# Laying out the context and three weight matrices by columns on the host, in a gated cross-attention and expert kernel

## The chip, the cores and the metric

The kernel runs on one core of a Trainium2 chip. The metric is device microseconds of one execution, the median of several runs. The engines are called TensorE (PE in the rows; PEld is its weight load), VectorE (DVE), ScalarE (ACT), GpSimd (POOL) and the DMA queue of the Sync engine (SP).

## What is computed

Inputs are `x` and a context, both (8, 512, 512) in float32: 8 batches of 512 rows and 512 features. Cut to what matters:

```python
n = layernorm(x); c = ctx_1024
s  = softmax((n @ Wq_c.T + bq_c) @ (c @ Wk_s.T + bk_s).T / sqrt(512)) @ (c @ Wv_s.T + bv_s)   # d = 0
t  = softmax((c @ Wq_s.T + bq_s) @ (n @ Wk_c.T + bk_c).T / sqrt(512)) @ (n @ Wv_c.T + bv_c)   # d = 1
g  = sigmoid(concat([s, t]) @ Wg.T + bg)
x  = x + tanh(g_xattn) * (g * s + (1 - g) * t)
m  = layernorm(x)
p  = softmax(m @ router_w + router_b);  e = argmax(p)
x  = x + tanh(g_ffn) * max(p) * (m @ expert_w[e] + expert_b[e])                                # 8 experts
```

## The kernel before

**Number format.** Every operand of a large product is kept as a pair, a high part (a rounded copy, made by ScalarE) and a low part (value minus high part, made by VectorE). `product` (L153) multiplies two pairs over four chunks of 128 in three passes: 12 matmuls of 128x512. The pairs live in an arena of nine slots of [128, 2, 4, 512]: `WG_S, A_X, A_C, CT, XT, WV_S, WV_C, WG_C, PAIRS` (L56). CT and XT hold the context and the normalised x of one batch with the features across the partitions, so they need the transposed inputs. WV_S, WV_C, WG_C and WG_S need the transposed weights.

**Steps.** The work of all engines is written out by hand as one list of steps (`opening_steps` L180, `steps_of_a_batch` L496, `steps_after` L584). Each engine walks the same list and does its part of each step, in that order; semaphores join them. A step is a kind and digits: Q10 is kind Q, direction 1, tile 0. Kinds: Q (queries, product with the folded matrix A = Wk.T Wq), S (scores, with the row maximum on VectorE and the exponential on ScalarE), NP (normalisation), V (values), PT (transposes of the probabilities), U (attended sum, into four banks), ND, G (gate), M, MX, BS, NM, NT, NR, LG, LR (mix, statistics and router logits of the batch before), RT, RK (ranks for the expert lists), XS, XN, XD, XT (x of the next batch: statistics, normalisation, a dot product, transposes), CD, CT (context of the next batch: a dot product, transposes). Only in the first batch come the steps of the weights: W (splits), AC, AD, A (products for the folded matrices) with AE (their eviction), SC (a scaled copy on ScalarE, added up by GpSimd, L361), FOLD0 to FOLD2 (sums over that, which the first scores and dot products need) and WT0 to WT15 (the transposed weights, four tiles each of WG_C, WV_S, WV_C, WG_S in this order, `LATE` L57).

The first batch runs as written out code, batches 1 to 6 in a hardware loop (L1132, L1245, L1437), the last again as written out code, and behind it 39 expert tiles.

**A CT, XT or WT step before.** Four transposes by TensorE into one bank (`transposes` L1003; CT L1085, WT L1082), a copy of the bank to the high part by ScalarE (L1199, L1209), a subtraction by VectorE to the low part (L1277, called at L1333 and L1337). In the loop CT0 stands behind Q13, CT1 and CT2 between the scores of direction 1, and CT3 between V11 and PT11. The source of CT is the same `in_tile` that CD reads; SP waits for both in front of the next load into it (`after_c` L834).

**WT loads before.** SP loads 16 tiles of 256 KB one after the other into four small tiles (`late_rows` L648, L935 to L940), each as soon as the transposes of the one four places before are done.

**Gates that the steps below touch.** V of the first batch waits for the low parts of WV (L1026), U00 for the second folded matrix (L1048), S00 for CT's low parts and FOLD2 (L1031 to L1033), FOLD1 and FOLD2 for GpSimd's additions (L471), PT10 for the normalised probabilities (L1040).

Of the kernel before, what the change touches and what calls it, by code (L numbers as in the profile page):

```python
# [73 lines left out]
def gated_attention_and_experts(nc, x, ctx_in, g_xattn, g_ffn, Wq_c, bq_c, Wk_s, bk_s, Wv_s, bv_s,  # L74
                                Wq_s, bq_s, Wk_c, bk_c, Wv_c, bv_c, Wg, bg, router_w, router_b,
                                expert_w, expert_b, out):
# [8 lines left out]
    with ExitStack() as top:  # L85
# [90 lines left out]
WT_ROWS = 4  # L176
# [15 lines left out]
def weights_part(nc, top, k, x1_dram, list_dram, w):  # L192
# [297 lines left out]
    part.nat_lo, part.scaled_up, part.fold_read = nat_lo, scaled_up, fold_read  # L490
# [114 lines left out]
def attention_part(nc, scope, top, k, x_rows, c_rows, x1_dram, x1_early, list_dram, expert_w,  # L605
# [163 lines left out]
    def tr_bank_of(step):  # L769
# [3 lines left out]
        if kind in ("M", "WT") or kind in ("NT", "CT", "XT") and rel == 0:  # L773
            return tr_bank[i % 2]
# [25 lines left out]
    def wait_readers(pe, b, step):  # L800
# [12 lines left out]
        elif kind == "CT":  # L813
            pe.wait_ge(ct_lo, per_batch(b + rel, i))
# [6 lines left out]
        elif kind == "RK":  # L821
            pe.wait_ge(ranks_read, b + rel + 1)
        elif kind == "WT":
            pe.wait_ge(wt_lo, i + 1)

    def sync(sp, weights_run, experts_run):
# [7 lines left out]
        def after_c(b, t):  # L834
            await_count(sp, waits_passed_sp, ct_tr, per_batch(b, t))
# [1050 lines left out]
```

## Time and profile before

| what | value |
|---|---|
| median of 3 runs | 1160.65 us (1157.68 to 1161.5) |
| the profiled execution | 1168.7 us, span 1166.9 us |
| mean granted TensorE clock | 0.999 |
| TensorE matmuls busy | 1146.8 us, 98% of the span |
| TensorE weight loads busy | 943.5 us, 81% |
| VectorE, ScalarE, GpSimd busy | 709.8, 458.8, 212.4 us (61, 39, 18%) |
| DMA | 90.64 MB, mean 78 GB/s |

The span reaches from the first to the last instruction of the profiled execution. "Busy" is the time in which at least one instruction of the engine is under way; matmuls overlap, so their durations add up to more than the time they take. In a timeline row the bracket at the end is idle time of the engine in front of the row, and who ended it.

### The profile page before, as it was taken

What the parts mean: (1) busy time and instruction counts of PE and PEld (TensorE: products, weight loads), DVE (VectorE), ACT (ScalarE), POOL (GpSimd) and SP (SyncE); (2) the same over time, 40 slices, a digit from 0 to 9 for tenths busy, and PEclk for the clock granted to TensorE, in tenths of its full rate; (3) what the DMA queues carried; (4) which work ended last, traced back from release to release, by engine and by line L of the source; (5) the groups of instructions that cost most, each with busy time, mean ns of one, the idle gap of its engine ahead of it and who ended that gap; (6) DMA issues with size and microseconds to landing.
All of it is one profiled execution on the core that took longest, in us unless ns stands there. A gap on an engine that the chain in (4) does not pass through costs nothing.

```text
span 1166.9 us, 18111 instructions
## 1 busy us (share of the span) xinstructions
PE 1146.8 (98%) x5933; PEld 943.5 (81%) x5933; DVE 709.8 (61%) x1494; ACT 458.8 (39%) x815; POOL 212.4 (18%) x339
## 2 busy tenths in 40 slices
PE   8999999999999999999999999999999999998998
PEld 7878888888888888888888888888888888876776
DVE  6666646564656565654576366646664667787565
ACT  5634413442343234432443234423442344553332
POOL 2400101020102000210011001101120102165564
PEclk9999999999999999999999999999999999999999
DMA  7141103011201020102011111112000322685683
GB/s 254 49 162 37 37 28 100 19 31 36 99 0 48 27 99 9 48 27 81 27 39 34 56 54 21 36 42 84 21 28 10 136 62 66 221 266 167 187 252 109
DMA packets 59445, 90.64 MB, mean 78 GB/s; under 512 B 20523, under 2 KB 21063, under 8 KB 59401
## 3 DMA queue, kind: packets, MB, share of 16 engines
q1 hardware_dynamic: 49232, 64.25, 18.2%
q0 software_dynamic: 7264, 19.20, 5.1%
q10 hardware_dynamic: 2904, 6.63, 1.6%
q8 instruction: 24, 0.39, 0.1%
q14 instruction: 21, 0.16, 0.0%
HBM read 62.77 MB, written 29.12 MB: 79 GB/s over the span
## 4 chain that ended last, share of the span: by engine, by line
PE 93%; issue 3%; SPq 2%; DVE 1%; ACT 1%; DMA 0%; another core or an unknown queue 0%; POOL 0%; POOLq 0%; DVEq 0%
PE mm L160 59%; PE u L1053 15%; PE tr L1005 8%; PE u L160 6%; PE tr L160 1%; PE mm L1834 1%; PE u L443 1%; SPq L1583 1%; PE tr L1107 1%; SPq L1584 1%; PE mm L485 0%; DMA probs<-in_L_ffn_expert_b 0%; SPq L1604 0%; SPq L1603 0%; DVE slot_as_f L1810 0%
## 5 line engine op out<-in xcount | busy, mean ns | idle before, releaser
L160 PE MATMUL mm<-arena 128*128 128x512 f32 x1536 | 374.2, 395 | 1.5 <-DVE arena L1277 1.4
L160 PEld LDWEIGHTS mm<-arena 128*128 128x128 f32 x1536 | 282.8, 188 | 58.6 <-DVE arena L1277 1.7
L1053 PE MATMUL u<-arena 128*128 128x512 f32 x768 | 189.8, 397 | 0.0
L160 PE MATMUL mm<-arena,q_pair 128*128 128x512 f32 x768 | 183.8, 394 | 0.0
L160 PEld LDWEIGHTS mm<-arena,q_pair 128*128 128x128 f32 x768 | 141.7, 188 | 28.7
L1053 PEld LDWEIGHTS u<-arena 128*128 128x128 f32 x768 | 140.0, 188 | 27.4
L1277 DVE TENSOR_TENSOR arena<-tr,arena 128x512 fp32r<-128x512 f32 x143 | 96.1, 686 | 36.6 <-ACT arena L1168 16.5
L1277 DVE TENSOR_TENSOR arena<-mm,arena 128x512 fp32r<-128x512 f32 x65 | 45.0, 692 | 91.6 <-ACT arena L1159 87.2
L1155 ACT ACTIVATE q_pair<-mm,c_col 128x512 fp32r<-128x512 f32 x64 | 44.1, 689 | 125.8 <-PE mm L160 122.6
L1278 DVE SCALAR_TENSOR_TENSOR q_pair<-mm,c_col,q_pair 128x512 fp32r<-128x512 f32 x64 | 48.1, 751 | 70.7 <-ACT q_pair L1155 69.1
L1159 ACT ACTIVATE arena<-mm 128x512 fp32r<-128x512 f32 x64 | 38.3, 599 | 128.8 <-PE mm L160 128.8
L160 PE MATMUL mm<-c2s_pair,arena 128*128 128x512 f32 x360 | 87.2, 392 | 0.0
L160 PE MATMUL mm<-q_pair,arena 128*128 128x512 f32 x360 | 86.4, 389 | 0.0
L1164 ACT ACTIVATE probs<-mm,neg_top 128x512 f32<-128x512 f32 x64 | 44.2, 690 | 102.4 <-DVE neg_top L1304 92.8
L160 PE MATMUL u<-arena,q_pair 128*128 x312 | 79.4, 405 | 1.3 <-DVE q_pair L1795 1.2
L1461 POOL TENSOR_SCALAR mv_x<-mv_x 128x1 f32<-128x1 f32 x28 | 12.6, 451 | 368.1 <-DVE mv_x L1344 368.1
L160 PEld LDWEIGHTS mm<-q_pair,arena 128*128 128x128 f32 x360 | 67.6, 188 | 14.0
L160 PEld LDWEIGHTS mm<-c2s_pair,arena 128*128 128x128 f32 x360 | 67.1, 188 | 13.8
L1461 POOL TENSOR_SCALAR stats<-stats 128x1 f32<-128x1 f32 x32 | 8.0, 248 | 355.9 <-DVE stats L1376 355.6
L1323 DVE SCALAR_TENSOR_TENSOR probs<-probs,u 128x512 f32<-128x512 f32 x32 | 22.0, 688 | 79.4 <-ACT probs L1191 79.2
L1191 ACT ACTIVATE probs<-mm,bg_half 128x512 f32<-128x512 f32 x30 | 20.7, 690 | 123.6 <-PE mm L160 123.6
L160 PEld LDWEIGHTS u<-arena,q_pair 128*128 128x128 f32 x312 | 57.9, 192 | 13.4 <-issue 2.0
(223 smaller groups left out, 1558.8 us busy)
## 6 DMA issues: line engine op xcount, KB each, us to landing
in_tile<-in_ctx SPq DMA_DIRECT2D x31, 256.0 KB, 2.7
x_tile<-in_x SPq DMA_DIRECT2D x29, 256.0 KB, 2.6
x_rows<-x_tile SPq DMA_DIRECT2D x29, 256.0 KB
in_tile<-in_x SPq DMA_DIRECT2D x28, 256.0 KB, 2.6
x_rows_early<-x_tile SPq DMA_DIRECT2D x28, 256.0 KB, 2.3
probs<-in_L_ffn_expert_b SPq DMA_DIRECT2D x21, 256.0 KB
slot_as_f<-in_L_ffn_expert_w SPq DMA_DIRECT2D x4, 1024.0 KB, 5.3
slot_as_f<-in_L_ffn_expert_w ACTq DMA_DIRECT2D x3, 1024.0 KB, 7.6
```

The lines of the kernel that those rows point to most:

```text
L160: last = pe.matmul(bank, lhsT(a, c), rhs(b, c), start=start and n == 0, stop=stop and n == C * len(PASSES) - 1)
L443: last = pe.matmul(bank[m][:], pair[0][0][:, a, i, m * P:(m + 1) * P], pair[0][1][:, b, i], start=i == 0 and n == 0, stop=i == C - 1 and n ...
L1005: last = pe.transpose(bank[:, tile(n)], block_of(n), ident[:])
L1053: last = pe.matmul(u_bank[m][:], v_pair[:, i % 2, a, tile(m)], pt_pair[:, i % 2, p], start=i == 0 and n == 0, stop=i == T - 1 and n == 2)
L1155: act.activation(q_pair[:, HI, i], bank[:], ACT.Identity, bias=c_col[:, d, i:i + 1]).then_inc(q_hi, 1)
L1159: act.activation(v_pair[:, i % 2, HI], bank[:], ACT.Copy).then_inc(v_hi, 1)
L1164: act.activation(probs[:, i], bank[:], ACT.Exp, bias=neg_top[:, d, i:i + 1], scale=SCALE, accum_out=p_sum[:, d, i:i + 1]).then_inc(exp_don ...
L1191: act.activation(probs[:, i], bank[:], ACT.Tanh, bias=bg_half[:, i:i + 1], scale=0.5).then_inc(tanh_done, 1)
L1277: return dve.tensor_tensor(to, bank, f32(hi), ALU.subtract)
L1278: return dve.scalar_tensor_tensor(to, bank, bias, f32(hi), ALU.add, ALU.subtract)
L1323: dve.scalar_tensor_tensor(mix, mix, 1.0, u_bank[i][:], ALU.subtract, ALU.mult).then_inc(nd_used, 1)
L1461: then(pool.tensor_scalar(rstd, var, EPS, None, ALU.add))
```

## The change

The host hands over the context transposed in each batch (`ctx_1024_by_columns`, beside the context itself) and `Wv_s`, `Wv_c` and `Wg` transposed (in place of the originals). A plain DMA puts them where TensorE's transposes and the two evictions put them before:

- `load_columns_of_c` loads the context of one batch, 1 MB, straight into the low half of the CT slot (for batch 0 of the WG_S slot). It waits until the last Q of direction 1 is done; in the loop it stands on SP behind `store_stats` and in front of `load_rest_of_x`.
- `load_late` loads each of the four weight blocks, 1 MB each, into the low half of its own slot (WV_S into the four small tiles), each behind a wait of its own.
- ScalarE copies from there to the high half, VectorE subtracts in place. TensorE's part of CT and WT, their banks and their waits are gone. SP's `after_c` waits for the dot product alone.
- CT0 to CT3 of the next batch move back in the list: behind U10, U11, U12 and U13. In the first batch, CT of batch 0 and all WT steps stay in their places.

The core of the diff (signatures, names of semaphores and argument lists left out):

```diff
@@ steps_of_a_batch
-    s += cur("Q", 1, 3) + load(6, 7) + nxt("CT", 0)
+    s += cur("Q", 1, 3) + load(6, 7)
     keep = lambda *ns: [("KC", 0, 0, n) for n in ns]
-    s += nxt("XN", 0) + cur("S", 1, 0) + prev("RK", 0) + nxt("CT", 1) + keep(0)
-    s += cur("S", 1, 1) + keep(1) + nxt("XD", 0) + cur("S", 1, 2) + nxt("CT", 2) + keep(2)
+    s += nxt("XN", 0) + cur("S", 1, 0) + prev("RK", 0) + keep(0)
+    s += cur("S", 1, 1) + keep(1) + nxt("XD", 0) + cur("S", 1, 2) + keep(2)
     s += cur("S", 1, 3) + keep(3) + cur("NP", 1, 3) + table(0) + nxt("CD", 2) + cur("V", 1, 0)
     s += nxt("XT", 0) + load(8) + cur("PT", 1, 0) + load(9)
-    s += cur("V", 1, 1) + load(10) + nxt("CD", 3) + nxt("CT", 3) + cur("PT", 1, 1) + table(1) + load(11, 12) + cur("U", 1, 0)
-    s += load(13) + nxt("XS", 1)
-    s += cur("V", 1, 2) + load(14) + nxt("XN", 1) + cur("PT", 1, 2) + table(2) + load(15) + cur("U", 1, 1) + nxt("XS", 2) + nxt("XD", 1)
+    s += cur("V", 1, 1) + load(10) + nxt("CD", 3) + cur("PT", 1, 1) + table(1) + load(11, 12) + cur("U", 1, 0)
+    s += load(13) + nxt("CT", 0) + nxt("XS", 1)
+    s += cur("V", 1, 2) + load(14) + nxt("XN", 1) + cur("PT", 1, 2) + table(2) + load(15) + cur("U", 1, 1) + nxt("CT", 1)
+    s += nxt("XS", 2) + nxt("XD", 1)
...
-    s += nxt("XS", 3) + prev("ID", 0) + nxt("XD", 2) + nxt("XT", 2) + nxt("XN", 3)
+    s += nxt("CT", 2) + nxt("XS", 3) + prev("ID", 0) + nxt("XD", 2) + nxt("XT", 2) + nxt("XN", 3)
...
-    s += cur("U", 1, 3)
+    s += cur("U", 1, 3) + nxt("CT", 3)
@@ attention_part
+    def columns_of_c(b, i):
+
+        slot = WG_S if isinstance(b, int) and b == 0 else CT
+        return k.slot_as_f32[slot][:, LO, i]
+
+    def late_raw(i):
+
+        return late_rows[i % C] if LATE[i // C] == WV_S else k.slot_as_f32[LATE[i // C]][:, LO, i % C]
@@ sync
         def after_c(b, t):
-            await_count(sp, waits_passed_sp, ct_tr, per_batch(b, t))
             await_count(sp, waits_passed_sp, c_dotted, per_batch(b, t))
+        def load_columns_of_c(b, first=False):
+            if first:
+                sp.wait_ge(weights.group_mm, C)
+            else:
+                await_count(sp, waits_passed_sp, q_mm, per_dir(b - 1, 1, C - 1))
+            to = k.slot_as_f32[WG_S if first else CT][:, LO]
+            sp.dma_start(to, ctx_columns[bass.ds(b, 1)].rearrange("o (c p) l -> p (o c) l", p=P)).then_inc(ct_loaded, 16)
+
+        def load_late(n):
+            place, w = LATE[n], late_weights[n]
+            if place == WV_S:
+                for c in range(C):
+                    sp.dma_start(late_rows[c], w[tile(c), :]).then_inc(wt_loaded[n], 16)
+                return
+            if place == WG_C:
+                sp.wait_ge(weights.nat_lo, 2 * C)
+                sp.wait_ge(weights.folded_col, C)
+            elif place == WV_C:
+                sp.wait_ge(weights.group_mm, 2 * C)
+            else:
+                sp.wait_ge(ct_lo, C)
+            sp.dma_start(k.slot_as_f32[place][:, LO], w.rearrange("(c p) o -> p c o", p=P)).then_inc(wt_loaded[n], 16)
...
         load_small()
+        load_late(LATE.index(WV_S))
+        load_late(LATE.index(WG_C))
+        load_columns_of_c(0, first=True)
         sp.wait_ge(in_loaded[0], loads_of("C", 0, 0))
-        sp.wait_ge(weights.group_mm, C)
         load_c(0, T - 1)
-        for n in range(4 * C):
-            if n == 11:
-                load_next(1, first=True)
-            if n >= WT_ROWS:
-                sp.wait_ge(wt_tr, n - WT_ROWS + 1)
-            sp.dma_start(late_rows[n % WT_ROWS], late_weights[n // C][tile(n % C), :]).then_inc(wt_loaded[n % WT_ROWS], 16)
-        sp.wait_ge(wt_tr, 4 * C)
+        load_late(LATE.index(WV_C))
+        load_late(LATE.index(WG_S))
+        load_next(1, first=True)
+        sp.wait_ge(wt_lo, C * (LATE.index(WV_S) + 1))
         load_first_residual(0)
         load_rest_of_c(1)
+        load_columns_of_c(1)
         load_rest_of_x(1)
...
             load_rest_of_c(b + 1)
             store_stats(b - 1)
+            load_columns_of_c(b + 1)
             load_rest_of_x(b + 1)
@@ tensor
-                elif kind == "WT":
-                    pe.wait_ge(wt_loaded[i % WT_ROWS], 16 * (i // WT_ROWS + 1))
-                    transposes(bank, lambda n: late_rows[i % WT_ROWS][:, tile(n)]).then_inc(wt_tr, 1)
-                elif kind == "CT":
-                    buf = place_of("C", bb, i)
-                    pe.wait_ge(in_loaded[buf], loads_of("C", bb, i))
-                    transposes(bank, lambda n: c_of(bb, i)[:, tile(n)]).then_inc(ct_tr, 1)
@@ scalar
+                elif kind == "CT":
+                    act.wait_ge(ct_loaded, 16 * (bb + 1))
+                    if first and rel == 0 and i == 0:
+                        act.wait_ge(weights.nat_lo, 4 * C)
+                        act.wait_ge(weights.scaled_up, 3 * C)
+                    act.activation(arena[:, CT, HI, i], columns_of_c(bb, i), ACT.Copy).then_inc(ct_hi, 1)
                 elif kind == "WT":
...
                         lists_filled()
+                        act.wait_ge(c_dotted, T)
                     if i == 0:
                         act.wait_ge(weights.scaled_up, C)
-                    act.wait_ge(wt_tr, i + 1)
-                    act.activation(arena[:, LATE[i // C], HI, :, tile(i % C)],
-                                   bank[:].rearrange("p (c t) -> p c t", c=C), ACT.Copy).then_inc(wt_hi, 1)
+                    if LATE[i // C] == WV_S and i % C == 0:
+                        act.wait_ge(weights.group_mm, 2 * C)
+                    act.wait_ge(wt_loaded[i // C], 16 * (C if LATE[i // C] == WV_S else 1))
+                    act.activation(arena[:, LATE[i // C], HI, i % C], late_raw(i), ACT.Copy).then_inc(wt_hi, 1)
@@ vector
+                elif kind == "CT":
+                    dve.wait_ge(ct_hi, per_batch(bb, i))
+                    low(arena[:, CT, LO, i], columns_of_c(bb, i), arena[:, CT, HI, i]).then_inc(ct_lo, 1)
                 elif kind == "WT":
                     dve.wait_ge(wt_hi, i + 1)
-                    low(arena[:, LATE[i // C], LO, :, tile(i % C)], bank[:].rearrange("p (c t) -> p c t", c=C),
-                        arena[:, LATE[i // C], HI, :, tile(i % C)]).then_inc(wt_lo, 1)
+                    low(arena[:, LATE[i // C], LO, i % C], late_raw(i),
+                        arena[:, LATE[i // C], HI, i % C]).then_inc(wt_lo, 1)
```

## Rows read from the trace of the kernel before

**Rows 1.** The page: TensorE's busy time, and its granted clock by slice.

```profile
PE 1146.8 (98%) x5933; PEld 943.5 (81%) x5933; DVE 709.8 (61%) x1494; ACT 458.8 (39%) x815; POOL 212.4 (18%) x339
...
PEclk9999999999999999999999999999999999999999
```

**Rows 2.** The page: the chain that ended last, by engine.

```profile
PE 93%; issue 3%; SPq 2%; DVE 1%; ACT 1%; DMA 0%; another core or an unknown queue 0%; POOL 0%; POOLq 0%; DVEq 0%
```

**Rows 3.** Windows by stage: us, busy (count) by engine, PEclk, DMA share, GB/s.

```profile
65.70:91.99 26.29, 26.29 (x133) 21.84 (x134) 15.74 (x32) 10.85 (x20) 0.00 (x0) 1.00 0.30 99
...
204.53:937.40 732.87, 732.87 (x3834) 605.76 (x3832) 428.21 (x932) 271.41 (x488) 84.80 (x174) 1.00 0.14 44
...
1060.00:1166.90 106.90, 94.56 (x452) 75.58 (x450) 65.15 (x117) 35.65 (x55) 60.73 (x58) 0.98 0.61 179
```

**Rows 4.** Line 1005: count, duration ns min/median/max, first and last start.

```profile
L1005 PE MATMUL tr<-ident,in_tile x236: 270/272/308, 41.9 to 880.7; 128*128 128x128 f32 x118
```

**Rows 5.** TensorE in time, loop, from Q13's end (start us, us, what).

```profile
225.97 0.60 PE L1005 MATMUL tr<-ident,in_tile 128*128 128x128 f32 x4
...
235.50 0.60 PE L1005 MATMUL tr<-ident,in_tile 128*128 128x128 f32 x4
...
238.71 1.52 PE L160 MATMUL mm<-arena 128*128 128x512 f32 x6
```

**Rows 6.** TensorE in time, last batch, S10 and V10.

```profile
958.80 2.88 PE L160 MATMUL mm<-arena,q_pair 128*128 128x512 f32 x12
...
970.14 2.88 PE L160 MATMUL mm<-arena 128*128 128x512 f32 x12
```

**Rows 7.** TensorE in time, loop, CT3 and PT11.

```profile
245.04 0.60 PE L1005 MATMUL tr<-ident,in_tile 128*128 128x128 f32 x4
245.48 0.60 PE L1005 MATMUL tr<-ident,probs 128*128 128x128 f32 x4
```

**Rows 8.** VectorE's lines 1348 and 1394, GpSimd's 361: ns min/median/max.

```profile
L1348 DVE CUSTOM_DVE_ANT_0 junk<-pairs_as_f,u_row,u_const x4: 752/1200/1824, 40.7 to 50.3; 128x512 bf16<-128x512 f32 x4
...
L1394 DVE TENSOR_TENSOR arena<-slot_as_f,arena x32: 681/684/694, 929.6 to 1015.6; 128x512 fp32r<-128x512 f32 x32
...
L361 POOL TENSOR_TENSOR slot_as_f<-slot_as_f x9: 1278/1297/1740, 33.3 to 44.9; 128x512 f32<-128x512 f32 x9
```

**Rows 9.** SP in time, the page's loads (KB, us to landing), ScalarE in time.

```profile
232.24 0.41 SPq L871 DMA_DIRECT2D x_rows<-stats  x1
...
slot_as_f<-in_L_ffn_expert_w SPq DMA_DIRECT2D x4, 1024.0 KB, 5.3
...
251.59 0.60 ACT L1159 ACTIVATE arena<-mm 128x512 fp32r<-128x512 f32 x1 [4.77 <-PE mm L160]
```

**Rows 10.** First batch in time: FOLD1, FOLD2, S00 on TensorE; GpSimd's additions.

```profile
37.57 0.35 PE L479 MATMUL mm<-slot_as_f 128*128 128x1 f32 x2 [0.38 <-issue]
...
46.44 0.95 PE L476 MATMUL mm<-slot_as_f 128*128 128x1 f32 x8
...
51.52 3.00 PE L160 MATMUL mm<-arena,q_pair 128*128 128x512 f32 x12
...
33.29 4.18 POOL L361 TENSOR_TENSOR slot_as_f<-slot_as_f 128x512 f32<-128x512 f32 x3 [14.98 <-ACT slot_as_f L295]
...
40.65 5.50 POOL L361 TENSOR_TENSOR slot_as_f<-slot_as_f 128x512 f32<-128x512 f32 x4 [0.26 <-ACT slot_as_f L295]
```

**Rows 11.** First batch's S phase in time: row maxima, WT7's subtraction, V00.

```profile
54.63 0.69 DVE L1300 TENSOR_REDUCE mx<-mm 128x1 f32<-128x512 f32 x1 [0.76 <-PE mm L160]
...
58.85 0.68 DVE L1300 TENSOR_REDUCE mx<-mm 128x1 f32<-128x512 f32 x1
...
62.46 0.68 DVE L1300 TENSOR_REDUCE mx<-mm 128x1 f32<-128x512 f32 x1
...
64.86 0.69 DVE L1277 TENSOR_TENSOR arena<-tr,arena 128x512 fp32r<-128x512 f32 x1 [0.74 <-ACT arena L1209]
...
65.70 3.01 PE L160 MATMUL mm<-arena 128*128 128x512 f32 x12
```

More of the change, by code:

```diff
@@ L71, in f32, with gated_attention_and_experts @@
     return ap.bitcast(F32)
-def gated_attention_and_experts(nc, x, ctx_in, g_xattn, g_ffn, Wq_c, bq_c, Wk_s, bk_s, Wv_s, bv_s,
-                                Wq_s, bq_s, Wk_c, bk_c, Wv_c, bv_c, Wg, bg, router_w, router_b,
-                                expert_w, expert_b, out):
+def gated_attention_and_experts(nc, x, ctx_in, g_xattn, g_ffn, Wq_c, bq_c, Wk_s, bk_s, bv_s,
+                                Wq_s, bq_s, Wk_c, bk_c, bv_c, bg, router_w, router_b,
+                                expert_w, expert_b, ctx_columns, Wv_s_columns, Wv_c_columns, Wg_columns, out):
     x_rows = x.rearrange("b l h -> (b l) h")
@@ L126, in gated_attention_and_experts @@
         with ExitStack() as scope:
-            attention = attention_part(nc, scope, top, k, x_rows, c_rows, x1_dram, x1_early, list_dram, expert_w,
-                                       (Wg[:, 0:H], Wv_s, Wv_c, Wg[:, H:2 * H]), weights)
+            attention = attention_part(nc, scope, top, k, x_rows, c_rows, ctx_columns, x1_dram, x1_early, list_dram,
+                                       expert_w, (Wg_columns[0:H, :], Wv_s_columns, Wv_c_columns,
+                                                  Wg_columns[H:2 * H, :]), weights)
         experts = experts_part(nc, top, k, x1_dram, x1_early, list_dram, out_rows, expert_b, attention)
@@ L489, in weights_part @@
     part = Part(sync, scalar, vector, gpsimd, tensor)
-    part.nat_lo, part.scaled_up, part.fold_read = nat_lo, scaled_up, fold_read
+    part.nat_lo, part.scaled_up, part.fold_read, part.folded_col = nat_lo, scaled_up, fold_read, folded_col
     part.group_mm, part.group_lo, part.router_split = group_mm, group_lo, router_split
@@ L660, in attention_part @@
     q_mm, v_mm, s_mm, u_mm, g_mm = sem("q_mm"), sem("v_mm"), sem("s_mm"), sem("u_mm"), sem("g_mm")
-    pt_tr, ct_tr, xt_tr, m_tr, nt_tr = sem("pt_tr"), sem("ct_tr"), sem("xt_tr"), sem("m_tr"), sem("nt_tr")
+    pt_tr, xt_tr, m_tr, nt_tr = sem("pt_tr"), sem("xt_tr"), sem("m_tr"), sem("nt_tr")
+    ct_loaded = sem("ct_loaded")
     lg_mm, rk_mm, gc_mm = sem("lg_mm"), sem("rk_mm"), sem("gc_mm")
     lg_read = sem("lg_read")
-    wt_loaded, wt_tr, wt_hi, wt_lo = [sem(f"wt_loaded{i}") for i in range(WT_ROWS)], sem("wt_tr"), sem("wt_hi"), sem("wt_lo")
+    wt_loaded, wt_hi, wt_lo = [sem(f"wt_loaded{i}") for i in range(C)], sem("wt_hi"), sem("wt_lo")
     ex_loaded, ex_hi, ex_lo = [sem(f"ex_loaded{i}") for i in range(E + 1)], sem("ex_hi"), sem("ex_lo")
@@ L721, in c_of @@
         if isinstance(b, int) and b == 0 and t == T - 1:
-            return k.slot_as_f32[WG_S][:, LO, 0]
+            return k.slot_as_f32[WG_S][:, HI, C - 1]
         return in_tile[:, place_of("C", b, t), 0:H]
+    def columns_of_c(b, i):
[3 more added lines that the diff above has]
+        return late_rows[i % C] if LATE[i // C] == WV_S else k.slot_as_f32[LATE[i // C]][:, LO, i % C]
     def x_is_loaded(engine, b, t):
@@ L772, in tr_bank_of @@
             return mm_bank[1]
-        if kind in ("M", "WT") or kind in ("NT", "CT", "XT") and rel == 0:
+        if kind == "M" or kind in ("NT", "XT") and rel == 0:
             return tr_bank[i % 2]
@@ L1192, in run @@
                                    scale=0.5).then_inc(tanh_done, 1)
-                elif kind in ("CT", "XT"):
-                    done, hi, to = (ct_tr, ct_hi, CT) if kind == "CT" else (xt_tr, xt_hi, XT)
-                    act.wait_ge(done, per_batch(bb, i))
-                    if first and kind == "CT" and rel == 0 and i == 0:
+                elif kind == "XT":
+                    act.wait_ge(xt_tr, per_batch(bb, i))
+                    act.activation(arena[:, XT, HI, :, tile(i)], bank[:].rearrange("p (c t) -> p c t", c=C),
+                                   ACT.Copy).then_inc(xt_hi, 1)
+                elif kind == "CT":
+                    act.wait_ge(ct_loaded, 16 * (bb + 1))
+                    if first and rel == 0 and i == 0:
                         act.wait_ge(weights.nat_lo, 4 * C)
                         act.wait_ge(weights.scaled_up, 3 * C)
-                    act.activation(arena[:, to, HI, :, tile(i)], bank[:].rearrange("p (c t) -> p c t", c=C),
-                                   ACT.Copy).then_inc(hi, 1)
+                    act.activation(arena[:, CT, HI, i], columns_of_c(bb, i), ACT.Copy).then_inc(ct_hi, 1)
                 elif kind == "WT":
@@ L1517, in attention_part @@
     part.x1_copied, part.stats_copied = x1_copied, stats_copied
-    part.tiles_read = (xt_tr, x_dotted, ct_tr, c_dotted)
+    part.tiles_read = (xt_tr, x_dotted, c_dotted)
     part.m_tr, part.probs = m_tr, probs
@@ L1877 @@
     arrays, args = {}, []
-    for name in _INS:
-        a = _np.ascontiguousarray(inputs[name])
-        arrays[f"in_{name}"] = a
-        args.append(nc.dram_tensor(f"in_{name}", a.shape, _mybir.dt.from_np(a.dtype), kind="ExternalInput").ap())
+    laid_out = [(f"in_{name}", _np.ascontiguousarray(inputs[name])) for name in _INS]
+    laid_out += [(f"in_{name}_by_columns", _np.ascontiguousarray(_np.swapaxes(_np.asarray(inputs[name]), -1, -2)))
+                 for name in _INS_BY_COLUMNS]
+    for name, a in laid_out:
+        arrays[name] = a
+        args.append(nc.dram_tensor(name, a.shape, _mybir.dt.from_np(a.dtype), kind="ExternalInput").ap())
     args.append(nc.dram_tensor("out", (B, L, H), _mybir.dt.float32, kind="ExternalOutput").ap())
```

25 lines of the change are left out of this document (10 added, 15 removed).

## The prediction, made before the changed kernel had run

> **What bounds the kernel now.** I read the page's busy times and slices first. TensorE's matmul row is busy 98% of the span at a granted clock of 9 tenths or more in every slice [rows 1], and the chain that ended last is TensorE for 93% [rows 2]. The windows by stage say more than the averages: from 204.53 to 937.40 us, six batches, TensorE is busy 732.87 of 732.87 us while VectorE is busy 428 and ScalarE 271; in the last 107 us it is busy 94.6, so only the ends have gaps [rows 3]. In the batch loop, therefore, whatever is taken out of TensorE's stream comes off the time, as long as no partner that it stops covering becomes late. In the first batch that has to be checked wait by wait.
>
> **What a removed group is worth.** A CT or WT step is four 128x128 transposes into one bank. Their rows say 272 ns each [rows 4], but they are pipelined, so what counts is the distance between starts. The same stretch of steps, Q13's end to V10's start, stands in the loop with CT0, CT1 and CT2 in it and in the last batch (which has no next one) without. In the loop it goes from 225.97 to 238.71, 12.74 us [rows 5]. In the last batch S10 starts at 958.80 and V10 at 970.14, 11.34 us, with the same four products and the same ranks step [rows 6]. The difference, 1.40 us, is three groups: 0.467 us each, some 0.35 of issue and 0.11 that the product behind transposes takes longer. CT3 stands next to PT11, so it costs only the distance to it, 245.48 - 245.04 = 0.44 us [rows 7]. One batch's CT steps: 1.40 + 0.44 = 1.84 us.
>
> Weighed against that: durations would give 192 x 0.272 = 52 us, where distances give 48 x 0.46 = 22. The Trainium skill ("TensorE: Matmul & The Clock Gate", Part 4: PE-mode transpose) gives about 275 ns for a transpose in a kernel's context; taken as a cost that would make 52.8 us. The pair of stretches decides for the distance.
>
> **Part by part.**
> - *CT of batches 1 to 7, in the loop's code.* 28 groups leave TensorE: 7 x 1.84 = 12.9 us. What they covered: with CT0 gone S10 follows Q13 at once, and its last third needs Q13's low half; in the last batch that same adjacency runs without a gap [rows 6]. S12 and S13 now also stand back to back, as there. In this phase VectorE loses three subtractions and TensorE 1.40 us, so its cover improves. I cost the loss at 0 and keep for the range one group per batch, 7 x 0.467 = 3.3 us.
> - *CT0 to CT3 moved behind U10, U11, U12 and U13 on ScalarE and VectorE.* Each is one ScalarE copy and one VectorE subtraction as before, now with SBUF sources. The expert weights are split by just these forms: the subtraction takes 684 ns [rows 8]. ScalarE is idle 4.77 us in front of V12's eviction, so CT0 fits there [rows 9]. CT3 puts 0.7 us in front of the ND steps, with TensorE busy on the gate products for some 22 us. Cost 0.
> - *The load of the columns.* One 1 MB transfer per batch on SP, behind the stores of the statistics, issued at 232.24 in the batch shown [rows 9]; the column load follows at about 233.3. A 1 MB expert load takes a median 5.3 us to land [rows 9], so it is there at about 239. ScalarE reaches CT0 at 246.8 (251.59 less the idle 4.77): 8 us of cover. The three x loads behind it on SP wait for steps that come later (XT0 after V10, then CD2 and CD3), so they are not held. The former wait for the transposes in front of the next loads falls away. 8 MB more over the kernel, where the loop moves 44 GB/s and has its DMA engines 14% busy [rows 3]. Cost 0; if the cover is gone, see the slower rival.
> - *The first batch, up to FOLD2.* Seven groups (WT0, WT1, CT0 to CT3, WT2) are worth 7 x 0.45 = 3.1 us on TensorE, but GpSimd gates two places. FOLD1 started at 37.57, 0.1 us after GpSimd's third addition ended (33.29 + 4.18 = 37.47) and after 0.38 us of idle: it can't come sooner, so WT0 is lost. FOLD2 started at 46.44 and needs the last addition, which ended at 40.65 + 5.50 = 46.15 [rows 10]. So FOLD2 gains at most some 0.3 us, plus 0.3 if GpSimd's own gap is closed, though five more groups ahead of it are gone. Only WT2 lies behind it. Best case: 0.5 + 0.4 = 0.9 us. Against it, the subtractions now read two SBUF operands while GpSimd adds: with one such operation beside it, VectorE took up to 1.82 us for a form that takes 0.75, and one of GpSimd's nine additions took 1.74 us instead of 1.30 [rows 8]. Six subtractions now fall between 35 and 46 us; at 0.1 to 0.4 us each GpSimd ends 0.6 to 2.4 us later. I take 0.7 us. Net at S00 (51.52 before): +0.2 us gained, between -1.5 and +0.9. The Trainium skill ("GPSIMD Engine Reference", 1. Specifications) says that GpSimd's SBUF interfaces are contended by VectorE instructions with two SBUF inputs; it speaks against this change, and the trace agrees. Without that rule the stretch would gain 0.9.
> - *The first batch's S phase.* WT3 to WT7 are five groups, 2.2 us. But V00 waits for WT7's subtraction: it ran from 64.86 to 65.55, and V00 started at 65.70 [rows 11]. Behind that stands a chain through ScalarE and VectorE: each row maximum started 3.2 to 4.2 us after the one before (54.63, 58.85, 62.46), where a product takes 2.73 us. In program order lie maximum, exponential on ScalarE, the WT copies behind it, their subtractions, next maximum; no link of it waits for a transpose. Taking 5 groups out of TensorE leaves it. Gain 0.1 us, at most 2.2.
> - *WT8 to WT15.* From V00 on TensorE has no idle time (26.29 of 26.29 us in the window behind it [rows 3]): 8 x 0.44 = 3.5 us, less some 0.3 because U00 starts close behind the second fold's last subtraction. 3.2 us.
> - *The weight loads.* WG_C and batch 0's columns are issued once the first matrices are split, near 25 us, and are needed at 35 and 43 us; two times 5.3 us lands them near 36 at the latest, and the first WT copy is ScalarE's, not TensorE's. WV_C and WG_S land long before WT8 and WT12. Cost 0, up to 1 us.
> - *Last batch and experts.* Nothing is removed; their waits are for things that move along with the last batch. 0.
>
> **Sum.** 12.9 + 0.2 + 0.1 + 3.2 = 16.4 us. Against the profiled execution's span of 1166.9 (1168.7 us with what lies around it) that is 1.4%. The median of the runs shown is 1160.65, 0.7% below the profiled one; at this size the scaling is worth 0.1 us. Forecast: 1160.65 - 16.4 = **1144.2 us**.
>
> **Rivals.**
> - *All 48 groups come off.* 22.1 us, 1138.6. For it: TensorE's 98%. Against it: the gates of FOLD2 and V00 [rows 10, 11]. Chance 0.14.
> - *A partner becomes late somewhere.* The opening loses 1.5 instead of gaining 0.2, and one group per batch is swallowed in the loop's S phase (VectorE has a dot product there that the last batch lacks): 16.4 - 1.7 - 3.3 = 11.4 us, 1149.2; either alone 1146 to 1147.5. Chance 0.16.
> - *The transposes cost their durations.* 52 us, 1108.5. The equal stretches speak against it. Chance 0.01.
> - *Slower: the column load lands late.* ScalarE waits in order at CT0, behind it stands V12's eviction, and TensorE stops at the next product into that bank. It needs landing later than 13.5 us after issue to be felt on ScalarE, another 4.8 us before it delays the eviction, and then 16.4 / 7 = 2.3 us per batch to eat the gain: decides at some 20.6 us from issue, four times 5.3. At 25 us it would cost 7 x (25 - 18.3) = 47 us less the 16: 1191. Chance 0.04.
> - *Nothing to be seen (under 3.5 us gained).* It would need two thirds of a batch's groups swallowed in every batch; also if the 3 runs' own spread of 3.8 us hides part. Chance 0.05.
>
> **How the numbers follow.** My forecast has 0.60. About 0.3% (3.5 us) is what a measurement of this kernel can tell from no change. Faster by more: 0.60 + 0.14 + 0.16 + 0.01 = 0.91; same 0.05; slower 0.04. The range reaches from just below the case with all groups, 1138, to the case with the partners late, 1150.
>
> **What would show it.** Right: six batches take 732.9 - 6 x 1.84 = 721.8 us with TensorE still busy throughout, and the distance of S10 to V10 is the last batch's 11.3 us; FOLD2 starts between 46 and 48 us with idle time in front of it; V00 still waits for a subtraction of WT7 near 65.5; GpSimd's additions last longer. Wrong: idle time of TensorE in every batch (then who released it is the answer), FOLD2 near 44 us, V00 near 61, ScalarE waiting for the transfer of the columns at CT0, or a batch that shrinks by less than 1.5 us.

## The result and the profile after

The changed kernel takes 1147.09 us (median of 4 runs, 1145.39 to 1149.16), the kernel before 1159.54 (4 runs, 1157.68 to 1161.5): a ratio of 0.9893, 95% interval 0.9867 to 0.9919, or 12.4 us less. The forecast was 16.4 us less, from 1160.65 to 1144.2. The profiled execution has a span of 1146.1 us. One of the six executions of e4 below took 1896.96 us at a mean granted clock of 0.556; it is left out of the times and ratios here.

The page's rows of the changed kernel: busy times, granted clock by slice, chain of waits by engine, and the new load (count, KB each, median us to landing).

```profile
PE 1126.0 (98%) x5741; PEld 925.1 (81%) x5741; DVE 708.2 (62%) x1494; ACT 460.8 (40%) x815; POOL 209.8 (18%) x339
...
PEclk9999999999999999999999999999999999999999
...
PE 88%; issue 3%; SPq 2%; POOL 2%; DVE 2%; DMA 2%; ACT 1%; POOLq 0%; ACTq 0%; DVEq 0%
...
slot_as_f<-in_ctx_by_columns SPq DMA_DIRECT2D x8, 1024.0 KB, 5.6
```

TensorE is as full as before [rows 1], but the chain that ended last goes through it for 88% instead of 93% [rows 2]: the rest now passes through GpSimd, VectorE and DMA. Where that is shows in the windows of TensorE (us, busy and count, granted clock, DMA share, GB/s), first six batches of the loop, then three stretches of the first batch.

```profile
203.76:925.42 721.66, 721.66 (x3733) 1.00 0.18 54
...
44.00:48.00 4.00, 1.93 (x10) 1.00 0.01 4
48.00:52.00 4.00, 4.00 (x15) 0.63 0.00 0
...
68.00:72.00 4.00, 3.37 (x10) 0.69 0.13 50
```

The six batches take 721.66 us (721.8 forecast) instead of those of [rows 3], without any idle time: the loop gives what it was to give. The first batch doesn't. Between 44 and 48 us TensorE is busy 1.93 of 4 us, and behind that the granted clock is 0.63 and 0.69, where the kernel before showed a full clock throughout its first batch.

The loop, on TensorE's timeline: S10 and V10, to be set beside [rows 5, 6].

```profile
225.01 2.88 PE L161 MATMUL mm<-arena,q_pair 128*128 128x512 f32 x12
...
236.35 2.88 PE L161 MATMUL mm<-arena 128*128 128x512 f32 x12
```

11.34 us, the very distance of the last batch in [rows 6]; it was 12.74. The column load and its use, SP's queue and ScalarE's copy for CT0 and eviction of V12:

```profile
232.12 0.40 SPq L895 DMA_DIRECT2D slot_as_f<-in_ctx_by_columns  x1
```

```profile
243.89 0.64 ACT L1225 ACTIVATE arena<-slot_as_f 128x512 fp32r<-128x512 f32 x1
248.84 0.60 ACT L1182 ACTIVATE arena<-mm 128x512 fp32r<-128x512 f32 x1 [4.32 <-PE mm L161]
```

Issued at 232.12, landed 5.6 us later by the median, first used at 243.89: 6 us of cover, and ScalarE still idles 4.32 us in front of V12's eviction. No ScalarE or TensorE wait goes back to this load.

The opening, on TensorE's timeline from FOLD0 to PT00 (the bracket is idle time in front and who ended it).

```profile
25.89 0.95 PE L476 MATMUL u<-slot_as_f 128*128 128x1 f32 x8
...
39.11 0.35 PE L479 MATMUL mm<-slot_as_f 128*128 128x1 f32 x2 [1.24 <-issue]
...
47.99 1.05 PE L476 MATMUL mm<-slot_as_f 128*128 128x1 f32 x8 [2.07 <-POOL slot_as_f L361]
...
50.30 4.32 PE L161 MATMUL u<-arena 128*128 128x512 f32 x12
54.46 8.32 PE L161 MATMUL mm<-arena,q_pair 128*128 128x512 f32 x36
63.64 3.03 PE L161 MATMUL mm<-arena,q_pair 128*128 128x512 f32 x12 [0.86 <-ACT probs L1187]
68.63 4.57 PE L161 MATMUL mm<-arena 128*128 128x512 f32 x12 [1.95 <-DVE arena L1304]
...
73.04 0.60 PE L1035 MATMUL tr<-ident,probs 128*128 128x128 f32 x4
```

In order: FOLD0, FOLD1, FOLD2, A13, the scores S00 to S02, S03, V00, PT00. A13 and its successor in the kernel before, on TensorE's timeline:

```profile
48.02 3.32 PE L160 MATMUL u<-arena 128*128 128x512 f32 x12
...
51.17 0.60 PE L1005 MATMUL tr<-ident,normed 128*128 128x128 f32 x4
```

Against these and [rows 10, 11] three things are new. FOLD2 waits 2.07 us for GpSimd. A13 behind it takes 4.16 us to its successor (50.30 to 54.46), where it took 3.15. V00 waits 1.95 us for the subtraction of WT7, and then takes 4.4 us itself. Both slow products lie in the windows with the low clock above. The wait in front of FOLD1 grew as well, from 0.38 to 1.24 us: the place of the transposes is empty, and FOLD1 comes 13.22 us behind FOLD0 instead of 12.85.

### The profile page after: what moved, and what is told of

It reads as the page before. It is cut to its first block, busy times and chain, and to the rows that moved or that the text cites. A ratio compares the mean times of both kernels' runs of the same rounds, so it can differ in the third digit from the quotient of the medians.

```text
span 1146.1 us, 17654 instructions
## 1 busy us (share of the span) xinstructions
PE 1126.0 (98%) x5741; PEld 925.1 (81%) x5741; DVE 708.2 (62%) x1494; ACT 460.8 (40%) x815; POOL 209.8 (18%) x339
## 4 chain that ended last, share of the span: by engine, by line
PE 88%; issue 3%; SPq 2%; POOL 2%; DVE 2%; DMA 2%; ACT 1%; POOLq 0%; ACTq 0%; DVEq 0%
PE mm L161 59%; PE u L1083 15%; PE tr L1035 6%; PE u L161 4%; PE tr L161 1%; SPq L1612 1%; PE tr L1130 1%; DMA in_tile<-x_rows,u_row 1%; SPq L1613 1%; POOL slot_as_f L361 1%; PE mm L1863 1%; POOL out L1692 1%; DMA pairs_as_f<-in_x 0%; DMA probs<-in_L_ffn_expert_b 0%; DVE slot_as_f L1839 0%
## 5 line engine op out<-in xcount | busy, mean ns | idle before, releaser
L161 PE MATMUL mm<-arena,q_pair 128*128 128x512 f32 x768 | 179.7, 391 | 0.9 <-ACT probs L1187 0.9
L1304 DVE TENSOR_TENSOR arena<-tr,arena 128x512 fp32r<-128x512 f32 x95 | 63.9, 685 | 20.2 <-ACT arena L1191 16.4
L1327 DVE TENSOR_REDUCE mx<-mm 128x1 f32<-128x512 f32 x64 | 44.2, 691 | 50.9 <-PE mm L161 50.8
```

The costliest lines, as they stand in the source:

```text
L161: last = pe.matmul(bank, lhsT(a, c), rhs(b, c), start=start and n == 0, stop=stop and n == C * len(PASSES) - 1)
L1304: return dve.tensor_tensor(to, bank, f32(hi), ALU.subtract)
L1327: then(dve.reduce_max(mx[:, d, i:i + 1], bank[:], axis=AX))
```

## Where the time went, by stage

Starts of the same steps in each profiled execution, subtracted (us). The labels are those of the experiments below; e0 is the changed kernel again. The experiments ran on three chips: e1 to e4 on one, e0 and e5 to e7 on a second, e8 and e9 on a third. The kernel before ran beside them on each and took 1167.5 to 1167.6 us, 8 us more than in the first comparison, so what is compared below is the ratio to it. e9 is e6 once more and left out here.

| stage | before | after | e0 | e1 | e2 | e3 | e4 | e5 | e6 | e7 | e8 |
|---|---|---|---|---|---|---|---|---|---|---|---|
| FOLD0 to FOLD2 | 21.72 | 22.10 | 22.05 | 22.09 | 22.08 | 21.27 | 21.70 | 22.08 | 21.71 | 24.47 | 21.73 |
| FOLD2 to S00 | 5.08 | 6.47 | 6.44 | 5.21 | 8.09 | 6.47 | 5.07 | 4.82 | 4.72 | 3.25 | 4.72 |
| S00 to V00 | 14.18 | 14.17 | 14.16 | 14.28 | 14.17 | 14.17 | 14.19 | 14.17 | 11.45 | 11.56 | 11.45 |
| V00 to PT00 | 2.85 | 4.41 | 4.05 | 2.85 | 2.83 | 4.26 | 2.85 | 2.83 | 2.85 | 2.81 | 2.85 |
| **FOLD0 to PT00** | **43.83** | **47.15** | **46.70** | **44.43** | **47.17** | **46.17** | **43.81** | **43.90** | **40.73** | **42.09** | **40.75** |
| PT00 to S10, batch 0 | 36.00 | 32.16 | 32.21 | 32.18 | 32.14 | 32.20 | 35.61 | 32.16 | 32.16 | 32.16 | 32.16 |
| S10 to the last gate | 895.15 | 882.38 | 882.46 | 882.59 | 882.76 | 882.66 | 882.76 | 882.43 | 883.25 | 883.47 | 883.26 |
| last gate to the end | 167.20 | 158.52 | 166.14 | 161.83 | 164.07 | 166.45 | 162.98 | 165.39 | 166.28 | 165.77 | 164.51 |

From before to after: +3.3 in the opening, -3.8 in the rest of the first batch, -12.8 up to the last gate, together -13.3 us, where the medians say -12.4. The last row scatters by 8 us between kernels that are equal there, and the kernel before has one profile, so the 8.7 us of its first two columns are not put down to the change. The start up to FOLD0 isn't in the table, because Q00 ran at the full clock in some profiles and at half in others, with the change and without (e2, e4, e8).

## The experiments

**e0: the changed kernel itself**, as a partner of e5 to e7 on their chip.

> The changed kernel itself, so that it stands beside the others on one chip. Expected: 1.1% below the kernel before, the same 47 us from FOLD0 to PT00 (43.8 before), with two slow stretches of TensorE or one.

1154.01 us, ratio 0.9879 (0.9864 to 0.9894). The opening is the same as in the first profile, both slow stretches included.

**e1: fillers at the old places.** A filler group is four transposes of the identity matrix into a bank that nobody reads. Twelve of them stand where WT0 to WT7 and batch 0's CT0 to CT3 stood. Only TensorE gets more work.

```diff
+FILLED = 8
...
+                elif (kind == "CT" and here == 0 and rel == 0) or (kind == "WT" and i < FILLED):
+                    for n in range(4):
+                        pe.transpose(tr_bank[i % 2][:, tile(n)], ident[:], ident[:])
```

> The changed kernel, with four transposes of the identity into a bank that nobody reads, at the old places of WT0 to WT7 and of batch 0's CT0 to CT3 (12 groups of 0.44 us put back on TensorE, everything else by columns). Theory 1 (in the opening TensorE waits for GpSimd and VectorE, and each time it has waited its clock falls to 1.2 GHz for a few us): the fillers cost nothing and keep it busy, no stretch has a granted clock below 0.95, V00 starts near 65.7 instead of 68.63, PT00 near 68.6 instead of 73.04; time 1147.1 - 4.5 = 1142.6 us. Rival 2 (the lateness comes from VectorE's subtractions with two SBUF operands beside GpSimd): FOLD2 stays at 48 and V00 at 67 or later; time 1145.5 to 1147. Rival 3 (the slow stretches are an accident of the one profiled run): they are gone here too, but the time is 1147 or, with 12 groups more on TensorE, up to 5 us longer.

1149.3 us, ratio 0.9853 (0.9830 to 0.9876) to the kernel before: 3 us below e0 by the ratios, with work put back. The intervals of the two overlap, and e0 ran on another chip, so the times alone don't prove it. The stages are clearer: PT00 comes 44.43 us behind FOLD0, 2.3 to 2.7 us sooner than in the two profiles of the changed kernel. FOLD2 doesn't come sooner (22.09): GpSimd sets it either way. What goes are the slow stretches, and V00's wait is down to 0.82 us. V00's start was expected near 65.7 and stood at 67.55, of which Q00's slow start in this profile is 1.4 us (4.31 us to FOLD0 instead of 2.87).

**e5: fillers in the waits alone.**

```diff
+                if here == 0 and (kind, rel, d, i) in (("FOLD", 0, 0, 2), ("V", 0, 0, 0)):
+                    fill(5)
```

> The changed kernel with fillers where it waits and nowhere else: five groups of four transposes into a free bank (1.8 us) in front of FOLD2's wait and five in front of V00's. Theory 1 (the wait itself lets the clock fall, and the fall costs 1.5 to 1.8 us each time): both waits shrink below 0.4 us, FOLD2 and V00 start within 0.2 us of where they start without the fillers, no granted clock below 0.95 behind them, PT00 comes 3 us sooner (44.2 us from FOLD0), the time is 3 us below the changed kernel's. Rival (the clock falls because there are fewer columns in these stretches as a whole, or at random): it falls in this kernel too and the time stays.

`fill(5)` issues five filler groups into the two transpose banks. TensorE's timeline (fillers, FOLD2, fillers, V00, PT00), and its windows.

```profile
45.95 2.34 PE L1040 MATMUL tr<-ident 128*128 128x128 f32 x20
48.20 1.05 PE L476 MATMUL mm<-slot_as_f 128*128 128x1 f32 x8
...
65.07 2.34 PE L1040 MATMUL tr<-ident 128*128 128x128 f32 x20
67.19 2.99 PE L161 MATMUL mm<-arena 128*128 128x512 f32 x12
70.02 0.60 PE L1035 MATMUL tr<-ident,probs 128*128 128x128 f32 x4
```

```profile
48.00:52.00 4.00, 4.00 (x23) 1.00 0.00 0
...
68.00:72.00 4.00, 4.00 (x21) 1.00 0.00 0
```

1151.09 us, ratio 0.9853 (0.9838 to 0.9868) against e0's 0.9879: 2.9 us by the medians, on the same chip. The intervals touch, but all four runs of e5 (at most 1151.73) lie below all four of e0 (at least 1151.9). FOLD2 stands 22.08 us behind FOLD0, as without fillers, so they took no time from anyone; the clock is 1.00 in both windows, A13 and V00 take their usual length, and FOLD0 to PT00 is 43.90. So the slow stretches go when TensorE has work through the waits. Whether the wait itself counts or the little work around it (FOLD2's matmuls have one column) is not separated: the fillers change both. The Trainium skill ("TensorE: Matmul & The Clock Gate", Part 4: PE-mode transpose) says that the full clock doesn't engage for transposes. These rows differ: twenty transposes in a row kept it at 1.00. Whether transposes would also raise it from the lower level no run shows.

**e3: the subtractions' second SBUF operand taken away.**

```diff
-                    low(arena[:, CT, LO, i], columns_of_c(bb, i), arena[:, CT, HI, i])
+                    raw = tr_bank[0][:] if here_first and rel == 0 else columns_of_c(bb, i)
+                    low(arena[:, CT, LO, i], raw, arena[:, CT, HI, i])
```

(and the same for WT0 and WT1). The low parts of batch 0's context and of half of WG_C are left out by this.

> The changed kernel, with the first operand of six subtractions of VectorE (WT0, WT1 and batch 0's CT0 to CT3) taken from a PSUM bank instead of SBUF. These low parts are then wrong values, nothing else is left out. If two SBUF operands hold up GpSimd: its nine additions take about 12.2 us together instead of 13.5, VectorE's CT0 and CT1 take 1.3 us together instead of 3.25, FOLD2 starts 1 to 1.3 us sooner against its first addition. Theory 1: the clock still falls behind FOLD2, so V00 gains about 1.2 us and the time 1 us, 1146. Rival 2: with this cause gone, V00 comes near 66 and the time is 1143 to 1144.

CT0's and CT1's subtractions on VectorE, and FOLD2 on TensorE:

```profile
44.03 1.29 DVE L1304 TENSOR_TENSOR arena<-tr,arena 128x512 fp32r<-128x512 f32 x2 [3.07 <-ACT arena L1225]
```

```profile
45.89 1.05 PE L476 MATMUL mm<-slot_as_f 128*128 128x1 f32 x8 [1.65 <-POOL slot_as_f L361]
```

The same two subtractions in the changed kernel, and GpSimd's nine additions beside them (in the kernel before the additions took 4.18, 2.53 and 5.50 us in three pieces, 12.21 together, the first and last in [rows 10]):

```profile
34.47 13.47 POOL L361 TENSOR_TENSOR slot_as_f<-slot_as_f 128x512 f32<-128x512 f32 x9 [16.22 <-ACT slot_as_f L295]
...
45.24 3.25 DVE L1304 TENSOR_TENSOR arena<-slot_as_f,arena 128x512 fp32r<-128x512 f32 x2 [1.38 <-ACT arena L1225]
```

3.25 us for the pair become 1.29. GpSimd's nine additions take 4.16 and 8.03 us in e3, 12.19 together instead of 13.47, and FOLD2 comes 0.8 us sooner behind FOLD0 (21.27), where 1 to 1.3 were expected. Both sides of the contention are real. It isn't the main term: FOLD2 to PT00 stays at 24.9 us, with both falls of the clock. The median, 1151.23, lies 2.8 us below e0's, which ran on another chip, and 1.8 below by the ratios (0.9864, interval 0.9842 to 0.9886, overlapping e0's); the stages explain 0.5 to 1.0 of it.

**e2: the moved loads held back.**

```diff
+        sp.wait_ge(weights.group_mm, C)
         load_late(LATE.index(WV_S))
```

> The changed kernel, with SP's loads of WV_S held back until the first folded matrix is done, as the first WT loads were before. In the profile after, TensorE waited 0.90 us instead of 0.54 in front of XT3 at 19.4 us, with the DMA engines 98% busy, and Q00's product behind it ran at a clock of 0.7. If the four loads that moved forward cause it: the wait is 0.5 us again, Q00 takes 2.9 us instead of 4.5, and the time is 1.5 us lower, 1145.5. Rival: Q00 stays slow or is slow by chance, the time stays at 1147.

1154.31 us, ratio 0.9888 (0.9864 to 0.9911), nothing gained: my suspicion falls. TensorE's timeline, XT3, Q00 and V00:

```profile
19.89 0.66 PE L1036 MATMUL mm<-ident,pairs_as_f 128*128 128x128 f32 x4 [0.90 <-ACT pairs_as_f L1242]
21.96 4.37 PE L161 MATMUL mm<-arena 128*128 128x512 f32 x12 [1.41 <-DVE arena L1305]
...
70.50 2.99 PE L161 MATMUL mm<-arena 128*128 128x512 f32 x12 [1.95 <-DVE arena L1305]
```

The wait in front of XT3 is still 0.90 us and Q00 still takes 4.2 us. The last row matters too: the same wait of 1.95 us in front of V00, and this time no fall. A wait of this length makes the fall possible, not certain. And the fall behind FOLD2 was longer here: FOLD2 to S00 took 8.09 us, with granted clocks of 0.59 and 0.55 in the windows 48 to 52 and 52 to 56 us, so the opening is as long as in the changed kernel (47.17 us) with one fall instead of two. A fall has no fixed price.

**e4: the loop alone.** The kernel before, with the columns of the context for batches 1 to 7 and CT0 to CT3 behind U10 to U13; batch 0 and the weights transposed on TensorE. The core (TensorE, then ScalarE; VectorE's subtraction likewise):

```diff
+                if kind == "CT" and rel == 1:
+                    continue
...
+                elif kind == "CT" and rel == 1:
+                    act.wait_ge(ct_loaded, LOADED_BEFORE + 16 * bb)
+                    act.activation(arena[:, CT, HI, i], columns_of_c(i), ACT.Copy).then_inc(ct_hi, 1)
```

> The kernel before, with the context by columns for batches 1 to 7 alone; batch 0's context and all weights are transposed on TensorE as before. Theory 1: the opening is that of before (V00 at 65.7, no stretch at a low clock), the batches shrink from 122.17 to 120.28 us: 7 x 1.89 = 13.2 us less than before, 1159.5 - 13.2 = 1146.3 us, so all of the change's gain is made here and what it does in the first batch is worth 1 us or less in sum. Rival 4 (the loop gives less over seven batches than the trace says, and the first batch gives the rest): 1149 or more.

1154.17 us (median of five), ratio 0.9893 (0.9872 to 0.9913), beside 0.9879 for the whole change: equal within the intervals. Everything that the change did to the weights and to batch 0's context is worth nothing that these intervals show: in the stages +3.3 us in front of PT00 and -3.4 behind it. TensorE's timeline, Q00 and FOLD2:

```profile
22.79 4.62 PE L160 MATMUL mm<-arena 128*128 128x512 f32 x12 [1.41 <-DVE arena L1297]
...
48.94 0.95 PE L476 MATMUL mm<-slot_as_f 128*128 128x1 f32 x8
```

This is the old opening, and Q00 is slow in it (12 matmuls in 4.6 us; it took 3.0 in the profile of the kernel before). So the fall at Q00 doesn't need the change.

**e6: WV first.** WV_S is what V00 waits for, WG_C isn't needed before the gate.

```diff
-LATE = (WG_C, WV_S, WV_C, WG_S)
+LATE = (WV_S, WV_C, WG_C, WG_S)
-        s += cur("S", 0, 0) + late(3) + [step_of("AE11")] + late(4) + cur("S", 0, 1) + late(5) + late(6)
-        s += cur("S", 0, 2) + late(7) + cur("S", 0, 3) + cur("NP", 0, 3)
+        s += cur("S", 0, 0) + cur("WH", 0, 0) + cur("WH", 0, 1) + cur("S", 0, 1) + cur("WL", 0, 0) + cur("WL", 0, 1)
+        s += cur("WH", 0, 2) + cur("WH", 0, 3) + cur("S", 0, 2) + cur("WL", 0, 2) + cur("WL", 0, 3) + cur("S", 0, 3)
+        s += cur("NP", 0, 3) + [step_of("AE11")]
```

WH is ScalarE's half of a WT step, WL VectorE's. The other twelve follow behind V01, the last of them in front of U12, V00 waits for the first four low parts instead of the first eight, and fillers stand at the old places of WT0, WT1 and batch 0's CT.

> The changed kernel in another order: WV_S and WV_C are split first, WG_C and WG_S later (their first use is the gate). Nothing of the weights falls between FOLD1 and FOLD2 any more; WV_S's four copies stand between S00 and S02 with their subtractions one score tile later, the second group's eviction AE11 behind the scores; fillers at the old places of WT0, WT1 and batch 0's CT. Theory: the first batch's scores no longer wait for ScalarE and VectorE in turn, 11.2 us from S00 to V00 instead of 14.2, FOLD2 0.3 us sooner, no slow clock: 6 us below the changed kernel, 3 us below the one with fillers alone. Rival (VectorE is simply full there): S00 to V00 stays above 13.5 us, nothing beyond the fillers' gain.

1148.73 us, ratio 0.9839 (0.9826 to 0.9853). VectorE's row maxima of the scores, in the changed kernel, and WT7's subtraction in front of the last:

```profile
57.45 0.69 DVE L1327 TENSOR_REDUCE mx<-mm 128x1 f32<-128x512 f32 x1 [2.31 <-PE mm L161]
...
61.70 0.68 DVE L1327 TENSOR_REDUCE mx<-mm 128x1 f32<-128x512 f32 x1
...
65.35 0.68 DVE L1327 TENSOR_REDUCE mx<-mm 128x1 f32<-128x512 f32 x1
...
67.79 0.69 DVE L1304 TENSOR_TENSOR arena<-diff,arena 128x512 fp32r<-128x512 f32 x1 [0.77 <-ACT arena L1237]
68.40 0.68 DVE L1327 TENSOR_REDUCE mx<-mm 128x1 f32<-128x512 f32 x1
```

and in e6, followed by FOLD2, V00 and PT00 on TensorE:

```profile
54.00 0.69 DVE L1334 TENSOR_REDUCE mx<-mm 128x1 f32<-128x512 f32 x1 [2.32 <-PE mm L161]
...
56.65 0.69 DVE L1334 TENSOR_REDUCE mx<-mm 128x1 f32<-128x512 f32 x1 [1.57 <-PE mm L161]
...
59.45 0.68 DVE L1334 TENSOR_REDUCE mx<-mm 128x1 f32<-128x512 f32 x1
...
62.23 0.68 DVE L1334 TENSOR_REDUCE mx<-mm 128x1 f32<-128x512 f32 x1
```

```profile
46.29 0.95 PE L476 MATMUL mm<-slot_as_f 128*128 128x1 f32 x8
...
62.46 3.01 PE L161 MATMUL mm<-arena 128*128 128x512 f32 x12 [0.41 <-DVE arena L1311]
65.31 0.60 PE L1036 MATMUL tr<-ident,probs 128*128 128x128 f32 x4
```

The maxima followed each other by 4.2, 3.6 and 3.0 us; now by 2.65, 2.8 and 2.8, near the 2.73 of a product. S00 to V00 falls from 14.17 to 11.45 us (11.2 expected), FOLD0 to PT00 to 40.73. These 2.7 us of the first batch had been a chain between ScalarE and VectorE and no transpose. Against e5 the medians give 2.4 us, where 3 were expected. S10 to the last gate is 0.8 us longer than in the others, and TensorE's timeline of e6 shows where, at the first gate tile of the first batch (its two halves):

```profile
133.35 2.88 PE L161 MATMUL mm<-c2s_pair,arena 128*128 128x512 f32 x12
136.81 3.04 PE L161 MATMUL mm<-q_pair,arena 128*128 128x512 f32 x12 [0.58 <-DVE q_pair L1312]
```

The second half starts 3.46 us behind the first, in e0 2.72 (140.11 and 142.83), behind a wait for VectorE that e0 doesn't have. That the weight steps moved back into this stretch cause it is likely, but no run tests it.

**e7: FOLD2 behind A13**, otherwise as e6.

> As the kernel before this one, with FOLD2 moved behind A13, so that TensorE has 2.7 us of product to do while GpSimd ends its additions, and three groups of fillers behind FOLD2. Theory: the wait in front of FOLD2 (2.1 us) goes, a new one of 1.2 us comes in front of S00 for FOLD2's readers on VectorE: 0.9 us less. Rival: VectorE's readers of FOLD2 are late for another reason (the subtractions of CT in front of them), and nothing is gained.

1150.19 us, ratio 0.9850 (0.9836 to 0.9863), 1.5 us above e6. FOLD2 to S00 shrinks by 1.5 us and FOLD0 to FOLD2 grows by 2.8: A13 now stands in front of it, and no wait went away, since e6 had none there that fillers didn't cover. The forecast gain of 0.9 us didn't come. From FOLD0 to S00 e7 takes 27.72 us and e6 26.43, 1.3 us more, and the three filler groups behind FOLD2 take just that (52.05 to 53.33 us): here they stood in no wait that the profile shows.

**e8 and e9: the start filled, and e6 again as its partner.**

> The kernel with WV first, with fillers also in the two waits of the start (8 transposes in front of XT3, 0.7 us, and 16 in front of Q00, 1.4 us), into a bank whose readers are done. In five of nine profiles so far, of kernels with this change and without, Q00 ran at half the clock behind these waits (4.5 us instead of 2.9). Theory 1: with the waits filled it never does, Q00 takes 2.9 us, and the median is up to 1 us lower than without (0.6 of 1.6 us). Rival (the fall at Q00 has another cause, since the waits are as long where it doesn't fall): Q00 is slow as often as before, no gain.

> The kernel with WV first once more, as the partner on the same chip: 1.6% below the kernel before.

(Q00 was slow in six of the ten profiles up to there, not in five of nine.) e8 1147.31 us, ratio 0.9826 (0.9809 to 0.9843); e9 1147.96, 0.9834 (0.9817 to 0.9850). TensorE's timeline of e8, fillers, fillers and Q00:

```profile
19.12 1.04 PE L1052 MATMUL mm<-ident 128*128 128x128 f32 x8
...
20.43 1.91 PE L1052 MATMUL mm<-ident 128*128 128x128 f32 x16
22.10 2.99 PE L161 MATMUL mm<-arena 128*128 128x512 f32 x12
```

Q00 takes its 2.8 us and the waits are filled, but e9's Q00 was fast as well, behind waits of 0.65 and 1.41 us, so the profiles don't tell; the medians differ by 0.7 us, less than the intervals. e9 couldn't tell: its wait in front of XT3 was one of the short ones. Over the eleven profiles without these fillers Q00 ran fast in all three with 0.54 to 0.69 us in front of XT3 (before, e6, e9) and slow in six of the eight with 0.82 to 0.92 us. Left open. Either kernel is faster than both originals: 1.7% below the kernel before, where the change as given was 1.2% below it on the chip of e0.

## Why the prediction was right, and where not

- **What a group is worth**, by distances and not by durations: right. S10 to V10 shrank by the 1.40 us forecast.
- **CT in the loop, 12.9 us**: 12.77 up to the last gate, and 0.39 for CT0 in front of S10 (36.00 - 35.61 in e4): 13.2 us. Its cover held everywhere; no group was swallowed in the S phase.
- **The move to U10 to U13 and the column load, 0**: right, 6 us of cover where 8 was forecast.
- **WT8 to WT15, 3.2 us**: 3.84 less CT0's 0.39 is 3.4.
- **S phase, 0.1 us**: right, 14.18 to 14.17 with five groups taken out, for the reason given.
- **Up to FOLD2, a net gain of 0.2 at S00, between -1.5 and +0.9**: here the prediction failed. FOLD0 to S00 went from 26.80 to 28.57, a loss of 1.8 us, just outside the bounds. That GpSimd gates FOLD1 and FOLD2 and gets later by contention was right (22.10 instead of 21.72; e3 puts the contention at 0.8 us where 0.7 stood). That the size came out near is partly luck: of the six subtractions only four ran beside the additions, two of them 0.9 to 1.1 us longer than their usual 0.69, and the last two, at 49.19 us, ran behind their end. Missing is a term: I counted a wait of TensorE as the time waited and nothing more. Behind the wait in front of FOLD2 and the one in front of V00 the granted clock fell to its lower level (1.2 instead of 2.4 GHz; 0.63 and 0.69 as means of 4 us), and the products behind ran long: 1.65 us from FOLD2 to S00 and 1.6 us at V00, by e5, which puts work into the waits and changes nothing else: 3.2 us against the profile of the changed kernel, 2.8 against that of e0, 2.9 in the medians.
- **The sum.** 13.2 + 3.4 - 3.3 = 13.3 us against 16.4 forecast. The 3.1 between them are the clock's 3.2 and the 0.4 that FOLD2 and V00 didn't give (+0.3 forecast, -0.1 measured with the waits filled, 43.90 against 43.83), less the 0.5 that the loop and WT8 to WT15 gave above their terms. The medians give 12.4; 1.1 us of the distance to 16.4 in them is that the kernel before has a median of 1159.54 over its four runs, and 1160.65 over the three that the forecast started from. The measured 1147.09 lay inside the range, 2.9 us above the forecast, but that was not the mechanism's doing alone: it also lies between 1146 and 1147.5, the prices of the rival "a partner becomes late" in one of its two places. Of that rival the opening's loss came about (-1.8 at S00 against -1.5), mostly for a reason that it didn't have, and the loop's didn't. The range covered a missing term of 3 us by its width.
- The rival "all 48 groups" failed at FOLD2 and V00, as forecast; the slower one never came near.

## What to carry to other kernels

Taking work off the engine that bounds a kernel gives its full price only where no wait takes its place; list the waits at the next gates before counting, and price a wait of TensorE with the slow products that can follow it, not by its length alone. Work that nobody reads, put into such a wait, can be worth more than it costs; put where there is no wait, it costs its time (1.3 us in e7). And where a step list joins engines, the step that gates an early consumer (WV here) belongs in front of one that gates a late one (WG), and two halves of a step on two engines needn't stand in the same place of the list.

## What the runs showed of the hardware

- The granted clock fell behind waits of 1.65 to 2.12 us: behind FOLD2's in four of four profiles that had it (after, e0, e2, e3), behind V00's in three of those four (not in e2, where V00 waited 1.95 us too). Behind FOLD1's wait of 1.24 us and S03's of 0.86 it didn't. At Q00, behind 0.54 to 0.92 and 1.41 us, it fell in six of eleven profiles.
- A fall cost 1.6 us behind FOLD2 in after, e0 and e3 and 3.3 in e2 (FOLD2 to S00, less e5's 4.82), and 1.2 to 1.6 us at V00.
- Twenty transposes of a constant in each of two waits kept the clock at 1.00 (e5).
- VectorE's subtraction of 128x512 takes 0.69 us; with two SBUF operands beside GpSimd's additions two of them took 3.25 us (1.57 and 1.75), and with a PSUM operand in the same place 1.29. GpSimd's nine additions took 13.47 us in the first case and 12.19 in the second.
